# Turning the relation counts of a graph kernel's adjacency stage: 64-column stationary one-hots in two column halves of TensorE

## The reference

```python
x = _layernorm(x + _L0_gnn_ref(...))   # attention over edges, softmax per destination
x = _layernorm(x + _L1_gnn_ref(x, edge_index, L1_gnn_W))
x = _layernorm(x + _L2_gnn_ref(...))   # gated messages, mean per destination
x = _layernorm(x + _L3_gnn_ref(x, edge_index, edge_type_64, ...))

# _L1_gnn_ref
new_H = segment_sum(H[src], dst);  out = relu((H + new_H) @ W)
# _L3_gnn_ref
rel_vec = rel_emb[clip(edge_type_ids, 0, 63)]
msg = (node_states[src] + rel_vec) @ W_msg.T + b_msg
agg = segment_sum(msg, dst) / max(degree, 1)
out = node_states @ W_self.T + b_self + agg
```

## Time and profile before

| | us |
|---|---|
| median of 3 runs | 1098.27 |
| lowest and highest | 1097.43, 1101.11 |
| profiled execution, its own time | 1098.61 |
| its span in the profile | 1096.8 |

### The profile page before, as it was taken

How to read it: one execution, slowest core, us unless ns; L and a number is a source line. 1 busy time by engine, 2 the same in 40 slices (tenths; PEclk the granted TensorE clock), 3 DMA queues, 4 the chain that set the end, 5 groups by cost and what they waited for, 6 DMA issues and landing times.

```text
span 1096.8 us, 28220 instructions
## 1 busy us (share of the span) xinstructions
PE 1009.4 (92%) x10463; PEld 865.8 (79%) x10463; DVE 907.4 (83%) x2226; ACT 722.1 (66%) x1559; POOL 217.8 (20%) x260
## 2 busy tenths in 40 slices
PE   3797979699999999995999999779999999989997
PEld 3343557599999999994677787759999999976765
DVE  6775999988998989988999999878787888766754
ACT  3466765555545555457899999567677776776554
POOL 4401340000000000000000000226676667610000
PEclk9899999899999999996999999889999999999999
DMA  6000020344444445410543344235444444357463
GB/s 158 1 1 1 4 68 3 110 147 149 165 128 157 157 139 168 135 64 21 168 130 128 126 124 127 75 113 141 126 142 138 121 138 133 116 188 237 145 171 116
DMA packets 79198, 128.27 MB, mean 117 GB/s; under 512 B 11147, under 2 KB 53206, under 8 KB 78828
## 3 DMA queue, kind: packets, MB, share of 16 engines
q1 hardware_dynamic: 73577, 115.20, 33.5%
q0 software_dynamic: 5056, 10.36, 3.8%
q10 hardware_dynamic: 426, 0.85, 0.3%
HBM read 101.50 MB, written 24.88 MB: 115 GB/s over the span
## 4 chain that ended last, share of the span: by engine, by line
PE 76%; DVE 12%; ACT 6%; issue 3%; DMA 1%; POOL 0%; POOLq 0%; SPq 0%; DVEq 0%; ACTq 0%
PE PS L2424 14%; PE PS L2618 14%; PE PS L2412 11%; PE PS L2601 8%; PE PS L2704 6%; PE PS L2529 5%; PE PS L2497 2%; PE PS L2250 2%; PE PS L2504 2%; PE PS L2263 2%; DVE vo L1592 2%; DVE ring L1588 2%; PE PS L2327 2%; ACT ring L1221 1%; ACT X L1160 1%
## 5 line engine op out<-in xcount | busy, mean ns | idle before, releaser
L1084 ACT CAST vo<-XT 128x768 f32<-128x768 bf16 (+1 forms) x218 | 180.3, 827 | 136.7 <-PE PS L2618 64.1
L920 POOL DMA_INDIRECT XT<-tab,ring x158 | 160.6, 1016 | 112.0 <-PE PS L2618 60.8
L2424 PE MATMUL PS<-vo 128*128 128x133 f32 x1300 | 175.9, 284 | 1.0 <-DVE vo L1694 1.0
L2424 PEld LDWEIGHTS PS<-vo 128*128 128x128 f32 x1300 | 157.2, 191 | 1.1 <-issue 1.1
L2412 PE MATMUL PS<-kp,ring 128*128 128x132 bf16 x1950 | 146.1, 220 | 3.3 <-DVE ring L1562 1.8
L2618 PE MATMUL PS<-vo 128*128 128x128 f32 x984 | 132.8, 279 | 0.0
L2412 PEld LDWEIGHTS PS<-kp,ring 128*128 128x128 bf16 x1950 | 125.3, 97 | 5.5 <-DVE ring L1562 1.9
L1570 DVE TENSOR_TENSOR XT<-iotab,XT 128x768 bf16<-128x768 bf16 (+1 forms) x218 | 119.8, 550 | 2.5 <-ACT XT L1077 2.5
L2618 PEld LDWEIGHTS PS<-vo 128*128 128x128 f32 x984 | 118.9, 191 | 3.0 <-issue 2.4
L2414 PE MATMUL PS<-SDP,ring 128*128 128x12 bf16 x650 | 110.0, 169 | 0.0
L1562 DVE TENSOR_SCALAR ring<-ring,pcolm 128x1664 bf16<-128x1664 bf16 x146 | 91.0, 651 | 19.1 <-PE PS L2601 15.5
(11 more groups left out here) (345 smaller groups left out, 2134.2 us busy)
## 6 DMA issues: line engine op xcount, KB each, us to landing
ring<-rows_d SPq DMA_DIRECT2D x146, 416.0 KB, 4.7
adj_d<-ring SPq DMA_DIRECT2D x100, 128.0 KB, 1.7
adj_d<-ring SPq DMA_DIRECT2D x75, 96.0 KB, 1.6
ring<-adj_d SPq DMA_DIRECT2D x11, 640.0 KB, 4.2
vo<-adj_d SPq DMA_DIRECT2D x9, 640.0 KB, 4.2
vo<-adj_d SPq DMA_DIRECT2D x8, 480.0 KB, 3.9
ring<-adj_d SPq DMA_DIRECT2D x7, 480.0 KB, 4.4
XT<-tab,ring POOLq DMA_INDIRECT x158
```

What stands on the lines that cost most here:

```text
L920: G.indirect_dma_start(far_rows[:, f % FBUF, :], None, tab[2], bass.IndirectOffsetOnAxis(ap=far_row[:, t:t + 1], axis=0)).then_inc(far_in[ ...
L1084: C.copy(ohd[:, k % 3, 0:n, :], ohb[:, k % 3, 0:n, :]).then_inc(hots_wide, 1)
L2424: T.matmul(bank(6 + b % 2)[:, 0:VW], ohd[:, k % 3, i, :], vals[:, k % 3, i, :], start=j == 0, stop=j == JN - 1).then_inc(scattered, 1)
```

## The change

The relation matmuls are turned around: the relation one-hots are stationary (64 columns) and the destination one-hots moving (128 columns). The result then has relations on the partitions. Even blocks d write partitions 0 to 63 of the bank and odd blocks partitions 64 to 127, so that two blocks lie below each other and the bank holds two times 128 columns. ScalarE copies the bank once at the group's end (all 128 partitions, 256 columns), now straight into `crel`. `rel_turned`, `rel_rows`, `crelT` and their semaphores go. SP stores each group's counts with two DMAs, one for each half of the partitions, at step 6 of the next group instead of step 9. TensorE's wait before the dense matmuls changes from `crelT_cp` to `crel_cp`, and the first of them also waits for the last bf16 cast (`adj_cp`).

```diff
-        crel = ring[:, 9472:9472 + 4 * 4 * P].bitcast(fp32).rearrange("p (r n) -> p r n", r=2)
-        crelT = ring[:, 11520:11520 + 4 * CT].bitcast(fp32).rearrange("p (r n) -> p r n", r=2)
+        crel = ring[:, 9472:9472 + 4 * 2 * P].bitcast(fp32).rearrange("p (r n) -> p r n", r=2)
...
             def crel_out(q):
-                w = even_width(q)
                 sp.wait_ge(crel_cp, q + 1)
-                sp.dma_start(crel_d[q][:, 0:w], crel[0:NREL, q % 2, 0:w]).then_inc(crel_io[q % 2], 16)
+                for t in range(2):
+                    sp.dma_start(crel_d[q].rearrange("r (a t p) -> r a t p", t=2, p=P)[:, :, t, :],
+                                 crel[NREL * t:NREL * (t + 1), q % 2, :].rearrange("r (a p) -> r a p", p=P)).then_inc(crel_io[q % 2], 16)
...
-                    if q and b == 9:
+                    if q and b == 6:
                         crel_out(q - 1)
...
-            def rel_rows(q):
-                w = even_width(q)
-                act.wait_ge(crel_tr, q + 1)
-                if q >= 2:
-                    act.wait_ge(crel_io[q % 2], 16 * (q // 2))
-                C.copy(crel[0:NREL, q % 2, 0:w], bank(7)[0:NREL, 0:w]).then_inc(crel_cp, 1)
-
...
-                    if q and b == 6:
-                        rel_rows(q - 1)
                 act.wait_ge(rel_mm, (q + 1) * NB)
-                C.copy(crelT[:, q % 2, 0:w // 2], bank(5 + q % 2)[:, 0:w // 2]).then_inc(crelT_cp, 1)
-            rel_rows(BANKS - 1)
+                if q >= 2:
+                    act.wait_ge(crel_io[q % 2], 32 * (q // 2))
+                C.copy(crel[:, q % 2, :], bank(5 + q % 2)[:, 0:2 * P]).then_inc(crel_cp, 1)
...
                     if q >= 2:
-                        pe.wait_ge(crelT_cp, q - 1)
-                    T.matmul(bank(5 + q % 2)[:, 0:even_width(q) // 2], zeros[0:1, 0:P], zeros[0:1, 0:even_width(q) // 2],
+                        pe.wait_ge(crel_cp, q - 1)
+                    T.matmul(bank(5 + q % 2)[:, 0:2 * P], zeros[0:1, 0:P], zeros[0:1, 0:2 * P],
                              start=True, stop=False, skip_group_check=True)
...
                 for d, blk in enumerate(both):
+                    to = bank(5 + q % 2)[NREL * (d % 2):NREL * (d % 2 + 1), d // 2 * P:(d // 2 + 1) * P]
                     _, d1, r1 = hots(ohs[:, s % 3, :], d)
-                    o = T.matmul(bank(5 + q % 2)[:, d * NREL:(d + 1) * NREL], d1, r1, start=False, stop=False, skip_group_check=True)
+                    o = T.matmul(to, r1, d1, start=False, stop=False, skip_group_check=True)
                     if b == 0:
                         _, d1, r1 = hots(ohx[:, q % 2, :], d)
-                        o = T.matmul(bank(5 + q % 2)[:, d * NREL:(d + 1) * NREL], d1, r1, start=False, stop=False, skip_group_check=True)
+                        o = T.matmul(to, r1, d1, start=False, stop=False, skip_group_check=True)
                 o.then_inc(rel_mm, 1)
-
-            def rel_turned(q):
-                pe.wait_ge(crelT_cp, q + 1)
-                pe.wait_ge(rc_cp, 1)
-                if q:
-                    pe.wait_ge(crel_cp, q)
-                for d in range(len(even(q))):
-                    o = T.transpose(bank(7)[0:NREL, d * P:(d + 1) * P], crelT[:, q % 2, d * NREL:(d + 1) * NREL], ident[:, :])
-                o.then_inc(crel_tr, 1)
...
-                if s >= NB and s % NB == 3:
-                    rel_turned(s // NB - 1)
-            rel_turned(BANKS - 1)
...
                 if i >= 5:
-                    pe.wait_ge(crelT_cp, BANKS)
+                    pe.wait_ge(crel_cp, BANKS)
                 if i == 0:
                     pe.wait_ge(rc_cp, 1)
+                    pe.wait_ge(adj_cp, NS)
```

More of the change, by code:

```diff
@@ L542, in gnn_kernel @@
         crel_cp = sem("crel_cp")
-        crel_tr = sem("crel_tr")
-        crelT_cp = sem("crelT_cp")
         crel_io = [sem(f"crel_io{n}") for n in range(2)]
@@ L630, in crel_stored @@
         def crel_stored(r):
-            return 16 * len(range(r, BANKS, 2))
+            return 32 * len(range(r, BANKS, 2))
         def on_act(s):
```

## The result

| | before | after |
|---|---|---|
| median of 4 runs, us | 1099.12 | 1128.05 |
| profiled execution, us | 1098.61 | 1126.16 |
| span, us | 1096.8 | 1124.4 |

The ratio is 1.0266 (95% interval 1.0242 to 1.0289): the change makes the kernel slower by 29 us. The sign and the mechanism were forecast; the time lies 8 us above the forecast of 1120, also above the forecast's own range of 1114 to 1126, and inside the range of 1109 to 1132 for 8 in 10.

The account below looks back on a forecast made before the run. TensorE was taken to bound the adjacency stage; longer steps (+10.9 groups 1 to 3, +13.5 groups 4 to 6), less transposes (-2.7) and with smaller terms, gave +22.5 us, so 1120 us; own range 1114 to 1126, 8 in 10 1109 to 1132.

Parts of the forecast that it names:

- TensorE binds the stage: Adjacency stage: TensorE sets the step, so anything added to its step costs nearly in full.
- The change of shape: Going between full-width and half-width matmuls around the relation matmuls costs about 0.09 us each way, twice a step.
- Entry: From the last adjacency matmul to the first relation matmul: 0.15 us, of which 0.09 is added.
- Exit: From the last relation matmul's start to the feature matmul: 0.06 + 0.09 = 0.15 us.
- Feature matmuls 0.34 apart: The gap between a step's two feature matmuls grows from 0.32 to 0.34 us.
- The halves overlap: Relation matmuls in the two column halves run side by side, with starts about 0.01 us apart in pairs.
- The spread of the starts: Relation matmuls of a four-block step start at 0, 0.01, 0.06, 0.07 us; first to last is 0.055 with three blocks.
- VectorE's slack: Groups 4 to 6: 1.5 us of the added time is hidden where TensorE already waited for VectorE.
- The signs I had named: Expected in the changed profile: four-wide steps of 1.14 to 1.18, three-wide 0.93 to 0.99, a stage 20 to 24 us longer.
- Transposes: 2.7: Taking away the fp32 transposes of the seven sets saves 2.7 us of TensorE time.
- Group 0: +2.7: The stage's first column group: 2.6 us for full-clock steps, less 0.9 of idle time absorbed, plus 1.0 for half-clock steps.
- Rival 2: Relation matmuls: halves overlap and changing the array's shape costs nothing, so faster by 8.5 us, 1090 us; chance 9%.

Follow-up runs that it names:

- e1: The changed kernel with 128 stationary columns instead of 64 in the relation matmuls, the extra rows unread, so each has the whole array: 1096.99 us.
- e4: The kernel before the change, with relation matmuls loading only 64 of the 128 stationary destination columns, all in one column half, nothing turned: 1138.92 us.
- e3: The changed kernel with its column halves, but the relation matmuls of five steps issued together, with seven one-hot buffers instead of three: 1093.41 us.
- e6: The changed kernel with only the first 64 of 128 destination columns moving in the relation matmuls: 1124.95 us.
- e5: The changed kernel with all relation matmuls in column half 0, so no second half to overlap with: 1144.25 us.
- e7: The changed kernel with the 64 stationary relation columns read side by side instead of every fourth: 1124.72 us.

## Why the prediction was right, and where it was short

*TensorE binds the stage, so a longer step costs in full.* Right. In groups 1 to 6 the steps got longer throughout and nothing took it up; ScalarE's and VectorE's waits grew instead.

*The change of shape costs about 0.09 on entry and exit.* Right, and shown from both sides: e1 takes it away with everything else turned, e4 brings it in with nothing turned, e3 divides the number by five. Entry 0.06 + 0.09 = 0.15: the last of four adjacency matmuls starts some 0.19 after 590.88, the relation matmuls begin at 591.22. Exit 0.15: measured 0.16. Feature matmuls 0.34 apart: measured 0.33 to 0.34. The rows for this were one-row and 32-column matmuls; the 64-column bf16 matmul behaves like them and not like the 64-column fp32 transpose. What the array does in the 0.09 no trace shows; it is the time between two starts. The split of the exit into a stream and a fixed 0.10 has a limit too. The one-row matmuls bear it out with longer streams: the next matmul comes 0.21 after one of 256 columns, 0.265 after 384 and 0.32 after 512 (e1, the last of them below), so 128 columns more add 0.05 each time and 0.10 is left over. But e6, with 64 columns, still has 0.16, and not the 0.13 that this would give:

```profile
570.71 0.39 PE L2472 MATMUL PS<-zeros 1*128 1x512 bf16 x1
571.02 0.41 PE L2485 MATMUL PS<-ring 128*128 128x128 bf16 x4
```

*The halves overlap.* Right (e5, 16 us).

*The spread of the starts.* This is the term that was mis-sized. I put 0, 0.01, 0.06, 0.07 and half of 0.03 for the first load; it is 0, 0.00, 0.11, 0.11, and with three blocks 0.11 instead of 0.055. For the first gap, too, I took the pace of a row of matmuls that is under way. By the sum of e6 and e7 the first gap is a load that nothing hides and then a whole stream. From first to last start it is 0.04 too little in steps of four and 0.055 in steps of three: 93 x 0.04 + 75 x 0.055 = 7.8 us, of which 168 x 0.015 = 2.5 were in the sum, so 5.3 short. The forecast was +22.5; with it, +27.8. Measured +28.9 by the medians, +27.6 by the profiled executions. That it comes out so near is in part luck, as the next two terms show.

*Where the forecast was short, by groups.* Its terms give 9.4 for groups 1 to 3, 10.7 for groups 4 to 6 and 2.4 for group 0 and the end of the stage. Measured are 11.9, 15.4 and, for all the rest of the execution, 0.4. So the starts (1.9 and 3.0 in these groups) explain most of what is missing in groups 1 to 3 and less than two thirds in groups 4 to 6. There a step of three blocks got 0.23 longer instead of 0.18 (1.013 instead of 0.780), and 75 such steps are 17.5 us, less 1.1 for the transposes: with 15.4 measured, about 1 us was hidden in VectorE's slack and not 1.5. Too little in the six groups and too much outside them partly cancel. The signs I had named say the same: steps of 1.14 to 1.18 and 0.93 to 0.99, where 1.19 and 1.01 came, and a stage 20 to 24 us longer, where its end moved by 28.7.

*Transposes: 2.7.* e1 is 2.9 us faster than the kernel before (0.0026 x 1100), but that is not the transposes alone, since its step of four is also 0.01 shorter. In its trace the gain is in groups 1 to 3 only (26.7, 26.7 and 26.4 us instead of 27.2, 27.3 and 27.0); groups 4 and 5 keep 21.3 and 21.4 us, since VectorE is level there. In the changed kernel TensorE is the longest everywhere, so there the full sum should apply; no run takes the transposes out by themselves.

*Group 0: +2.7.* From its first adjacency matmul to its last identity matmul 37.9 us instead of 35.3: +2.6. This is no confirmation. e1, whose steps are no longer, took 36.8 there; its granted clock was 0.62 from 524 to 526 us and 0.77 from 526 to 530, where the kernel before had 1.00. Group 0 began 1.2 us earlier in the changed kernel and ended 1.4 later.

Rival 2, faster by overlap without a cost of changing, had 9%. The Trainium skill, "TensorEngine Tiling (Array Packing)", recommends the swap under When to Use Tiling and has up to 2x under Theoretical Speedup. The pairs come near this 2x from the third on: 0.061 for two, where e1's full-width matmuls take 0.056 each, and 0.056 for two in e7; the step has only two pairs. The Trainium skill, same page, Key Properties, says that changing the mode drains the TensorE. The trace agrees that a change costs time, 0.09 us on the way in and 0.10 on the way out.

## What to carry to other kernels

Half-width matmuls pay for themselves only in runs: on this kernel a visit to the narrow shape costs about 0.25 us (0.09 in, 0.05 for the first load, 0.10 out, 0.02 behind), while a pair saves about 0.04 (0.06 instead of half of 0.20). So count the pairs per visit: by these gaps I estimate that about six are needed. The changed kernel had two and e3 has ten; nothing between was run. Where an odd number of blocks leaves a place in a pair empty, more are needed: e3 gained nothing in the groups of three. And collect them over several steps if buffers allow. If an operand only has to be turned to save transposes, load unread columns along and stay at full width (e1). A look for every narrow or one-row matmul between wide ones in an existing trace gives the price of the change before anything is built. What it does not give is the first gap behind the change, unless such a row stands in the trace.

## What the runs showed that I had not expected

- In a row of pairs each pair of 128-column matmuls starts 0.06 after the last, nearly twice the full-width rate (twice in e7), but the first gap behind a change is 0.11, and it shrinks to 0.08 both with half the moving columns and with a load that is read side by side (e6, e7).
- The gap from the last narrow matmul to the next wide one is 0.16 with 128 and with 64 moving columns, 0.15 in e7 and 0.17 in e4.
- In the first step of a group of the changed kernel, matmuls of the two halves start out of the program's order, side by side.
- A full-width load of which only half the columns are wanted is as quick as the one before (0.19 for four matmuls in e1 against 0.20). Narrowing a load cost 39 us where nothing else changed (e4). The load rows have medians of 0.11 for 128 columns read every fourth (e1), 0.14 for 64 read every fourth and 0.11 for 64 side by side (e7).
